# Two-layer adaLN network: attention scores for four row groups at a time in a ring of six banks, and expert tiles that live in one bank

## The reference, cut to what matters

```
for each sequence b (4 of them, 512 tokens each):
    h  = layernorm(x_b), shifted and scaled by the adaLN vectors
    q, k, v = h @ Wq.T, h @ Wk.T, h @ Wv.T   # 16 heads, two maps per head: 32 maps of width 8
    p  = softmax(q k^T / sqrt(8)), causal    # for each of the 32 maps
    o  = p[map 1] @ v - lambda_h * p[map 2] @ v ;  o = rmsnorm(o) ; x_b += gate * (o @ Wo.T)
    h  = layernorm(x_b), shifted and scaled
    every token picks 2 of 16 experts
    shared = (silu(h Ws1 + bs1) * (h Ws11 + bs11)) @ Ws2 + bs2          # hidden width 512
    expert = (silu(h W1 + b1) * (h W11 + b11)) @ W2 + b2                # hidden width 256, per picked expert
    x_b += gate * (shared + sum over the 2 picks of weight * expert)
```

## Time and profile before

| | |
|---|---|
| median of 3 runs | 1538.91 us (1535.56 to 1539.24) |
| the profiled execution's own time | 1543.92 us |
| its span, first to last instruction | 1542.2 us |
| busy: PE, DVE, ACT, POOL | 1138.1, 841.2, 608.2, 467.0 us |
| mean granted clock of TensorE | 0.79 |

### The profile page before, as it was taken

The page is one execution under the profiler, slowest core; times in us unless marked ns, Lnnn a source line. Parts: engine busy times, 40 slices in busy tenths (PEclk is TensorE's granted clock), DMA queues, the critical chain, the costliest instruction groups (busy, mean ns, idle before and its releaser), DMA issues.

```text
span 1542.2 us, 17520 instructions
## 1 busy us (share of the span) xinstructions
PE 1138.1 (74%) x5780; PEld 645.5 (42%) x5780; DVE 841.2 (55%) x1927; ACT 608.2 (39%) x1353; POOL 467.0 (30%) x661
## 2 busy tenths in 40 slices
PE   6353446956768968888888888986888979885762
PEld 3131123433434533333334345653455644563551
DVE  1586888588862436544444546656556555244332
ACT  3343343543443431333243336543345623661241
POOL 0201624525437220112124131245221362344202
PEclk9675767978989986667566779988789967896696
DMA  6000000000000010000000023410123301350352
GB/s 194 1 0 1 0 1 0 1 1 1 1 0 0 1 62 0 1 1 1 0 1 0 1 75 94 118 44 21 50 65 114 98 26 49 110 166 26 118 161 71
DMA packets 53883, 64.65 MB, mean 42 GB/s; under 512 B 6544, under 2 KB 38304, under 8 KB 53792
## 3 DMA queue, kind: packets, MB, share of 16 engines
q1 hardware_dynamic: 51744, 59.33, 13.1%
q0 software_dynamic: 2048, 4.20, 0.9%
HBM read 52.83 MB, written 10.68 MB: 41 GB/s over the span
## 4 chain that ended last, share of the span: by engine, by line
PE 51%; DVE 22%; issue 9%; ACT 8%; POOL 6%; DMA 3%; SPq 0%; DVEq 0%; POOLq 0%; ACTq 0%
PE banks L779 6%; PE banks L719 6%; DVE MX L1234 4%; PE banks L738 4%; PE banks L700 3%; PE banks L675 3%; PE banks L678 3%; PE banks L765 3%; PE banks L520 3%; PE banks L741 3%; PE banks L653 2%; PE banks L658 2%; PE banks L688 2%; DMA wg<-in_ffn_dram 2%; PE banks L573 2%
## 5 line engine op out<-in xcount | busy, mean ns | idle before, releaser
L1234 DVE TENSOR_REDUCE MX<-banks 128x2 f32<-128x1024 f32 (+3 forms) x176 | 197.6, 1126 | 133.9 <-PE banks L741 129.6
L1514 ACT ACTIVATE PT<-banks 128x768 f32<-128x768 f32 (+1 forms) x192 | 168.4, 881 | 235.5 <-PE banks L765 230.2
L1668 POOL TENSOR_SCALAR_AFFINE_SELECT PT<-PT 128x256 f32<-128x256 f32 x256 | 102.2, 412 | 416.2 <-ACT PT L1514 415.8
L738 PE MATMUL banks<-KS,QS 32*128 32x512 f32 (+3 forms) x512 | 105.3, 460 | 48.1 <-DVE KS L1224 13.8
L700 PE MATMUL banks<-w,hid 128*128 128x128 f32 x512 | 79.7, 304 | 70.9 <-DVE hid L1179 70.9
L765 PE MATMUL banks<-QS,KS 32*128 32x256 f32 (+3 forms) x512 | 101.0, 441 | 25.7 <-DVE MX L1234 12.2
L1183 DVE SCALAR_TENSOR_TENSOR sil<-sil,yh 128x256 f32<-128x256 f32 (+1 forms) x108 | 50.2, 465 | 123.2 <-ACT sil L1461 122.3
L700 PEld LDWEIGHTS banks<-w,hid 128*128 128x128 f32 x512 | 70.1, 209 | 110.8 <-DVE hid L1179 98.1
L779 PE MATMUL banks<-PT,VA 128*17 128x512 f32 (+3 forms) x1024 | 110.7, 535 | 0.0
L738 PEld LDWEIGHTS banks<-KS,QS 32*128 32x128 f32 x512 | 50.8, 218 | 123.2 <-issue 39.5
L1179 DVE TENSOR_TENSOR hid<-banks,sil 128x512 f32<-128x512 f32 x64 | 43.9, 687 | 79.9 <-PE banks L678 75.6
(11 more groups left out here) (244 smaller groups left out, 2238.3 us busy)
## 6 DMA issues: line engine op xcount, KB each, us to landing
wg<-in_ffn_dram SPq DMA_DIRECT2D x92, 386.0 KB
xg<-xs SPq DMA_DIRECT2D x20, 256.0 KB, 2.9
yb<-ysb SPq DMA_DIRECT2D x20, 256.0 KB, 3.8
w<-in_ffn_w_dram SPq DMA_DIRECT2D x12, 256.0 KB, 5.9
xs<-zt SPq DMA_DIRECT2D x1, 1472.0 KB, 10.8
x<-in_L_attn_x_dram SPq DMA_DIRECT2D x4, 256.0 KB, 5.0
out_dram<-x SPq DMA_DIRECT2D x16, 64.0 KB, 1.5
wmod<-in_L_wmod_dram SPq DMA_DIRECT2D x2, 384.0 KB, 4.3
```

Source lines behind the costliest of these rows:

```text
L738: e.matmul(p4[:, k, m, :], QS[lo:lo + 32, (t0 + m) % 12, 128 * qb:128 * qb + 128], KS[lo:lo + 32, (t0 + m) % 12, 0:nk], start=(m == 0), st ...
L1234: v_mx.at(e.tensor_reduce(MX[n % 2][:, s0:s0 + nm, 2 * pair:2 * pair + 2, 24].rearrange("p s i -> p i s"), p4, AX.X, ALU.max, negate=True))
L1514: a_p.at(e.activation(PT[q % 3][:, 2 * pair:2 * pair + 2, :], where["score", q, pair][:, :, 0:n], ACT.Exp, scale=ISQ8))
L1668: ins = e.affine_select(out=pt, in_=pt, compare_op=ALU.is_ge, fill=0.0, base=0, pattern=[[0, 2], [1, 128]], channel_multiplier=-1)
```

## The change

- `score` and `top` are issued for all four row groups in one job: two pairs of banks are taken, and the matmuls go round the four row groups. The counts of matmuls, reductions and exponentials stay. ACT and DVE still work by pairs; the second pair of a `score` is planned 1.2 units after the first, of a `top` 1 unit.
- The ring has six banks (0 to 5), four while the shared expert accumulates in bank 5.
- A tile of a picked expert, and a unit of the shared one, has one bank for both products; a tile's output also goes there, and `keep` copies each tile's 128 columns on its own. The bank is bank 6 for n < 3, and one of the ring for n = 3. ACT starts when both products are done. `down` is planned 4.5 units after `up`, `keep` 5.7.
- The shared expert has 8 units of 256 columns, 2.6 units apart.
- Tiles are 5.2 units apart for n = 0 and 1, 4.8 for n = 2, 2.4 for n = 3. DVE's `up` is 3 late instead of 4.
- `posi` has two buffers, so that positions of the next sequence are written before the rows of this one are collected.

```diff
-    step = 3.9 if n < 3 else 2.4
+    step = (5.2, 5.2, 4.8, 2.4)[n]
...
-    for j in range(4):
-        table += [(e + 60 + 5 * j, ("up", 1, n, j)), (e + 72 + 4 * j, ("down", 1, n, j))]
+    for j in range(SHARED):
+        table += [(e + 60 + 2.6 * j, ("up", 1, n, j)), (e + 66 + 2.6 * j, ("down", 1, n, j))]
...
-            table += [(t, ("up", 1, n, 4 + j)), (t + 6, ("down", 1, n, 4 + j))]
+            table += [(t, ("up", 1, n, SHARED + j)), (t + 4.5, ("down", 1, n, SHARED + j)), (t + 5.7, ("keep", n, j))]
...
             def take_pair(key):
-                i = (ring[0] + 1) // 2 * 2 % 4
+                i = (ring[0] + 1) // 2 * 2 % size[0]
                 ring[0] = i + 2
...
+                    if n < 3:
+                        i, ps = 6, take(6)
+                        where["unit", u] = ps
+                    else:
+                        i, ps = take_ring(("unit", u))
+                    for w, at, cols in parts:
+                        mm = e.matmul(ps[:, at:at + cols], w, h, start=True, stop=True)
                     p_p3.at(mm)
-                    busy[4] = [(v_hid, u + 1)]
+                    busy[i] = [(v_hid, u + 1)] if j < SHARED else [(a_ys1, TILES * n + j - SHARED + 1)]
...
+                    if j == 0:
+                        size[0] = 4
+                        where["shared", n] = take(5)
...
             def score(q, pair):
+                if pair:
+                    return
                 t = q // 3
                 pe.wait_ge(v_qs, 4 * (t // 4) + 4)
-                i = take_pair(("score", q, pair))
+                slots = [take_pair(("score", q, k)) for k in range(2)]
                 for kb, c0, n in STEPS[q % 3]:
-                    for k in range(2):
-                        lo = 64 * pair + 32 * k
-                        mm = e.matmul(bank[i + k][:, c0:c0 + n], KS[lo:lo + 32, t % 12, 128 * kb:128 * kb + 128],
-                                      QS[lo:lo + 32, t % 12, 128 * kb:512], start=True, stop=True,
+                    for k in range(4):
+                        mm = e.matmul(bank[slots[k // 2] + k % 2][:, c0:c0 + n],
+                                      KS[32 * k:32 * k + 32, t % 12, 128 * kb:128 * kb + 128],
+                                      QS[32 * k:32 * k + 32, t % 12, 128 * kb:512], start=True, stop=True,
                                       skip_group_check=True)
...
-                    v.wait_ge(d_coll, 128 * n)
-                    v_pos.at(e.tensor_copy(posi[:, :, :], posf[:, :, :]))
+                    v.wait_ge(d_coll, 128 * (n - 1))
+                    v_pos.at(e.tensor_copy(posi[n % 2][:, :, :], posf[:, :, :]))
...
-            def keep(n, c):
-                k, m = c % 2, len(CHUNKS[c])
-                a.wait_ge(p_y, 64 + UNITS[1] * n + 4 + CHUNKS[c][-1] + 1)
-                a.wait_ge(d_ys[k], 16 * (3 * n + c // 2))
-                a_ys1.at(e.activation(ysb[k][:, 0:m, :].rearrange("p c d -> p (c d)"), bank[5][:, 0:128 * m], ACT.Copy,
-                                      scale=0.5))
+            def keep(n, j):
+                c = j // 4
+                u = 64 + UNITS[1] * n + SHARED + j
+                a.wait_ge(p_y, u + 1)
+                a.wait_ge(d_ys[c % 2], 16 * (3 * n + c // 2))
+                a_ys1.at(e.activation(ysb[c % 2][:, j % 4, :], where["unit", u][:, 0:128], ACT.Copy, scale=0.5))
```

More of the change, by code:

```diff
@@ L63 @@
     PE=dict(norm=2.0, top_t=4.0, o_back=2.5),
-    DVE=dict(top=2.0, top_t=6.0, qk_in=2.0, up=4.0, down=1.0, route=2.0, place=0.0, w_o=2.0, rms=2.5),
-    ACT=dict(score=1.0, qk_in=1.0, v_in=1.0, norm=3.0, turn=1.0, up=1.5, keep=1.0, rms_t=1.0, route=4.0, gate_t=1.0),
+    DVE=dict(top=2.0, top_t=6.0, qk_in=2.0, up=3.0, down=1.0, route=2.0, place=0.0, w_o=2.0, rms=2.5),
+    ACT=dict(score=1.0, qk_in=1.0, v_in=1.0, norm=3.0, turn=1.0, up=1.5, rms_t=1.0, route=4.0, gate_t=1.0),
     POOL=dict(score=2.5, o_norm=1.5, w_o=3.0, stat=1.5, moe_x=1.0),
@@ L84, in front_table @@
         for s0 in range(0, 4, NM[qb]):
-            for pair in range(2):
-                table.append((t, ("top", b, h, qb, s0, pair)))
-                t += step
+            table += [(t, ("top", b, h, qb, s0, 0)), (t + 1, ("top", b, h, qb, s0, 1))]
+            t += 2 * step
         table.append((t, ("top_t", b, h, qb)))
@@ L340, in build @@
         posf = sb("posf", [128, 2, 4])
-        posi = sb("posi", [128, 2, 4], mybir.dt.uint32)
+        posi = [sb(f"posi{i}", [128, 2, 4], mybir.dt.uint32) for i in range(2)]
         gt_ = sb("gt_", [128, TILES, 16])
@@ L683, in down @@
                 pe.wait_ge(v_hid, u + 1)
-                if l and j >= 4:
-                    t = TILES * n + j - 4
-                    ps = take(5) if j % 4 == 0 else bank[5]
+                if l and j >= SHARED:
+                    w = wg[(TILES * n + j - SHARED) % 4]
                     for fh in range(2):
-                        mm = e.matmul(ps[:, 128 * (j % 4):128 * (j % 4) + 128], hid[u % 3][:, 128 * fh:128 * fh + 128],
-                                      wg[t % 4][:, 512 + 128 * fh:640 + 128 * fh], start=(fh == 0), stop=(fh == 1),
-                                      skip_group_check=True)
+                        mm = e.matmul(where["unit", u][:, 0:128], hid[u % 3][:, 128 * fh:128 * fh + 128],
+                                      w[:, 512 + 128 * fh:640 + 128 * fh], start=(fh == 0), stop=(fh == 1))
@@ L691, in down @@
                     p_y.at(mm)
-                    busy[5] = [(a_ys1, 6 * n + (j - 4) // 4 + 1)]
                     return
-                ex, fh = (j // 2, j % 2) if l == 0 else (0, j)
-                end = fh == (3 if l else 1)
-                iy = 5 if l else 3
-                ps = take(iy) if fh == 0 else bank[iy]
-                w2 = ws2[:, fh, :] if l else w2_0[:, ex, fh, :]
-                for i in range(4):
-                    mm = e.matmul(ps[:, 128 * i:128 * i + 128], hid[u % 3][:, 128 * i:128 * i + 128], w2,
-                                  start=(fh == 0 and i == 0), stop=end and not l, skip_group_check=True)
@@ L708, in down @@
+                ex, fh = j // 2, j % 2
+                ps = take(3) if fh == 0 else bank[3]
+                for i in range(4):
+                    mm = e.matmul(ps[:, 128 * i:128 * i + 128], hid[u % 3][:, 128 * i:128 * i + 128], w2_0[:, ex, fh, :],
+                                  start=(fh == 0 and i == 0), stop=(fh == 1), skip_group_check=True)
                 p_y.at(mm)
-                if l == 0:
-                    busy[iy] = [(a_yt, 8 * n + ex + 1)]
-                else:
-                    busy[iy] = [(v_acc, 5 * n + 1)]
+                busy[3] = [(a_yt, 8 * n + ex + 1)]
@@ L822, in _ @@
             pe.wait_ge(s_layer0, 4)
-            for i in (0, 1, 2, 3, 6):
+            for i in range(7):
                 busy[i] = []
```

173 lines of the change are left out of this document (92 added, 81 removed).

## The result

The changed kernel takes 1578.18 us (median of 4 runs, 1574.99 to 1584.08) against 1537.24 us for the kernel before: a ratio of 1.0271, 95% interval 1.0232 to 1.031. It is slower by 41 us; I had forecast 1523 us, faster. The profiled execution took 1574.99 us, its span is 1573.3 us, 31.1 us more than before.

The account below looks back on a forecast made before the run. PE's own work was taken to bound the halves, chains across engines after 1365 us, weight loads the last stretch. -25 - 2 + 26 - 15 = -16 us on 1543.9 gave 1528, in median terms 1523 us; 8-in-10 range 1470 to 1572.

Parts of the forecast that it names:

- part 2: Ring term: four-wide jobs wait for both pairs of banks, 4 us more per half, 12 us before 905 us (0 to 30).
- part 1: Four row groups for `top` and `score` in the time of two: 90 us of PE time saved, at the least nothing.
- I leave the clock as it is.: Whole kernel: PE's granted clock taken as unchanged, lower where PE waits, perhaps higher elsewhere; ends +-10 us.
- 579 to the first tile of n = 0: Stretch from 579 to 905 us: packing gain less ring waits and one-bank shared units, -25 us, ends -50 and 0.
- Part 3, the tile in one bank: Tile chain with both products in one bank: 6.4 us a tile in n = 0 and 1, ends 5.6 and 7.5.
- From 905 to 1306: Stretch with tiles of n = 0 and 1 beside attention: 399 us against 401, -2, ends -39 and +49.
- After 1306: Stretch 1306 to 1446 us, half 7 and the tiles behind it: one-bank tiles lengthen it, +26 us, ends +12 and +50.
- The last stretch: From 1446 us, tiles of n = 3: weight buffers return sooner, 2.4 us a tile, -15 us, ends -23 and 0.
- the rival at 1474: Rival: tiles cost only their PE work, 5.6 us each and 4.5 after 1365; 1474 us, chance 0.24.
- The slower one: Rival: one-bank loop holds attention up, `up` waiting for `keep` on bank 6, 7.1 us a tile; 1571 us, chance 0.26.
- The drains of the banks become the bound: Rival: DVE's reductions and ACT's exponentials bound the halves, only in bursts; 1541 us, no chance of its own given.
- the job of 1.30 times: Alternative for `top` and `score`: four row groups take 1.30 times two, saving 63 us instead of 90; 1550 us.

Follow-up runs that it names:

- e2: The changed kernel with `score` and `top` taken back to pairs, ring of six and one-bank tiles kept: 1500.16 us, ratio 0.9685 to the kernel before.
- e12: e2 with a ring of four banks instead of six until the shared expert of n = 0 is done: 1575.14 us, ratio 1.0193.
- e7: e2 with the tiles of n = 2 from the twelfth on in banks of the ring, 3 units apart: 1471.05 us, ratio 0.9532.
- e14: The changed kernel with eight useless bf16 products ahead of each four-wide job of halves 0 and 1: 1570.02 us, ratio 1.0212.
- e10: e2 with DVE's row maxima read over only half of the keys: 1461.74 us, ratio 0.9473 (two runs).
- e9: The changed kernel with `top` taken back to pairs and only `score` four wide: 1535.98 us, ratio 0.9959.
- e15: e7 with four useless bf16 products ahead of each pair of halves 0 and 1: 1479.57 us, ratio 0.9623.

## Why the prediction was wrong

**The step that failed** is the first one: "So whatever takes PE time out of the halves counts in full, as long as nothing new makes PE wait", together with the term of part 2 that was to price what is new, "I take 4 us more per half". The PE time of the two lines did go, as I said (busy 103 forecast, 102.5 measured). But ACT and DVE drain by pairs at their old pace, so the second pair of banks of a four-wide job is held while the first is drained, and PE waits until two pairs are free before it starts the next such job, often until both of the job before are drained. At the same ring, four-wide jobs leave PE idle for 35.5 us in halves 0 and 1 and pairs for 8.9: 13 us a half and not 4. I had counted the 4 us from the kernel before, with its ring of four, and there the term looks better than it is: PE idles for 35.7 us instead of 25.2 in halves 0 and 1, 5 us more a half, because the ring of six took 16 us of idle time away and the four-wide jobs put 27 in. That the two nearly cancel is luck. Over the first three halves it is 24 us, inside my 0 to 30.

Beside the tiles the same wait is larger, since `down` and `up` stand behind the waiting job, and there I had no such term beyond my tile period. From the first exponential of half 3 to that of half 7 PE idles for 65 us more than before, and its busy time falls by 9 us and not by 42. That is the largest miss: from the first tile of n = 0 to that of n = 2 the kernel takes 59 us more than before, where I had said 2 us less. e2 takes as long there as the kernel before (402.3 and 401.7 us). In halves 3 to 5 (by first exponentials) the changed kernel loses 50 us to e2. In all, -90 us forecast for part 1 became +90 (0.059) for four-wide jobs against pairs.

**Part 2, the ring as such.** I priced it as a cost that comes with four-wide jobs, and never asked what six banks do for pairs, though that is half of the edit. e12 against e2: 1.0193 - 0.9685 = 0.051, some 78 us, for four banks instead of six until the shared expert of n = 0 is done. The earlier trace rows had what it could be won from: clock 0.67, 45 us idle in 622 to 905.

**"I leave the clock as it is."** Over halves 0 and 1 the clock went from 0.66 to 0.79 with the change, and to 0.84 in e2. An estimate from busy time and clock by stretches: before the first exponential of half 3 the higher clock gives the changed kernel some 46 us, which is why 579 to the first tile of n = 0 came out at -48 us and not at -25, in spite of 35 us more of idle time. Behind that it takes some 32 us back (0.86 to 0.82 in halves 3 to 6, 0.91 to 0.71 from there to the last exponential). In sum that is some 14 us, and over the whole span the clock is 0.799 where it was 0.79: my end of +-10 us was nearly right for the sum, but by cancelling, and wrong for each stretch.

**Part 3, the tile in one bank.** Forecast 6.4 us a tile in n = 0 and 1, measured 7.67 and 6.84 (the earlier trace rows give 4.58 and 4.31 before). With pairs it is 6.34 and 6.07. That 6.4 is near this is no confirmation, since I walked through the order with four-wide jobs in it. By the unit, 6.34/5.2 = 1.22 us against 4.58/3.9 = 1.17 before: with pairs this stretch costs about what it did. What the loop alone costs beside attention no run shows. From 905 to 1306 I said -2; the two rows of the table for n = 0 and 1 give +59, and e2 +7. After 1306 I said +26 and got +36 (e2: +43); the mechanism was right and the size too small, because the tiles of n = 2 took 5.48 us and I had 5.6 in half 7 but 4.8 behind it. e7 takes 24 us of it away.

**The last stretch** came as forecast: -15 said, -16.1 measured, 2.4 us a tile said, 2.32 measured; the DMA share goes from 0.48 to 0.60. Two sums of mine were off and change nothing: 22.5 x (2.4 - 3.0) is -13.5 and not -15, and in the rival at 1474 the stretch from 1306 to 1446 comes, by its own 4.5 us a tile, to 13 + 14 - 5 = +22 and not +14, so that it stands at 1482.

**The rivals.** The slower one named 1571 us and the time was 1578, but that is in good part luck: its place was only half right. Its loop was to be `up` waiting for `keep`; that wait is 30.8 us in all, and nearly as large in e2 (28.0), as is that of `down` for `hid` (54.0 and 47.1). What the changed kernel has beyond e2 is `score` waiting for MX and `top` for PT, which I had under "The drains of the banks become the bound", at 1541. I dismissed that one by the busy shares of DVE and ACT in the earlier trace rows and by their sum of 51 us a half. The Trainium skill ("TensorEngine Tiling (Array Packing)", PSUM Bottleneck) warned of it, and the runs bear it out: DVE and ACT are busy for no more than 53% and 42% of halves 0 and 1 (71.27 and 56.09 of 135), and their drains are the bound all the same, because what is short is not their time but banks. Four row groups did go in the time of two, so the job of 1.30 times, worked out from the 3.07 of the Trainium skill ("TensorE: Matmul & The Clock Gate", Part 3, measured speedup), is refuted by the 0.80 and 0.50 us above.

What stays open: how much of the 0.041 that packing still costs with halved maxima is exponentials and how much the order; and what the granted clock follows. The runs show that useless products raise it, and that it rose with the ring of six and with halved maxima; they do not show a rule, and the idle share is not one.

## What to carry to other kernels

Price a wider job by the time its output banks are held, and not by the engine's time that it saves: where the reader's pace is unchanged, a job that takes all its banks at once empties the pipe that smaller jobs kept full. When a change has several parts, ask of each what it does alone; here the ring of six with pairs, and the ring for the later tiles, give 4.7%, and the packing costs 0.059 of the time of before. Where the granted clock is low, look at the clock of each stretch in every run, and not only at idle time: in these two halves 16 us fewer of idle time came with 32 us less of busy time for the same instructions. That is one case and no factor to carry: in e14, with the useless work in it, 9 us less of idle time came with 9.5 us in all.

## What the runs showed of the hardware that I had not expected

- The same 688 matmuls of halves 0 and 1 take 141.6 us of PE's busy time at a granted clock of 0.66 and 109.5 at 0.84.
- The clock does not follow the idle share of PE. At 8% idle it was 0.84 in e2 and 0.97 in e10, at 15% 0.66 before and 0.76 in e9, and at 21%, with gaps up to 1.8 us, 0.95 in e14.
- 271 useless bf16 matmuls in halves 0 and 1 of the kernel before raise the clock there from 0.66 to 0.89 and shorten the kernel by 1.5%. In e15, where only 8.9 us of 118 were idle, they raise it from 0.84 to 0.94, and the two halves still grow by 3 us.
- Four row groups of 32 rows and 512 columns take 0.80 us at half clock, as two do (0.79), and 0.50 us at full clock, as two do.
